# Four graph layers on one core: in the GAT walks SyncE copies 12 of turn 54's 14 columns row by row, and the staging of gather indices goes

## The chip, the cores and the metric

One NeuronCore of a Trainium2 chip runs the whole program. The metric is device time in microseconds, the median of several executions; lower is better. The engines are TensorE, VectorE (DVE), ScalarE (ACT), GpSimd (POOL) and SyncE (SP), each with its own queue of instructions; 16 DMA engines move data between the HBM and the on-chip memory (SBUF).

## The reference

Four graph neural network layers are applied in turn to 6250 nodes with 128 features and 100,000 edges (`src`, `dst`, sorted by `dst`), each with a residual and a layer norm:

```
x = layernorm(x + L0(x, src, dst))                  # gated sum of x[dst]-x[src]
x = layernorm(x + L1(x, src, dst, edge_weight))     # 4-head attention, aggregated at src
x = layernorm(x + L2(x, edge_index, edge_attr))     # 8-head attention with edge bias, and a feed-forward
x = layernorm(x + L3(x, edge_index))                # two GAT layers, 4 heads each
```

A GAT layer computes `h = x @ W`, a score for each edge and head `e = leaky_relu(a_src(h)[src] + a_dst(h)[dst])`, a softmax of `e` over the edges of one `dst`, and the sum of `h[src] * alpha` over them. Each node also counts as a neighbour of itself.

## The kernel before, in words

The program has five phases of edge work (`ph` 0 to 4; phases 3 and 4 are the two GAT layers) and a last, sixth pass over the nodes. A phase begins with dense work on the nodes, in 7 groups of 7 x 128 nodes: it reads the sums of the phase before, normalizes, multiplies by the weights and writes two tables to HBM: `table[ph]`, one row a node with what an edge needs of its `src` (in the GAT phases 136 floats, 544 bytes: 4 heads of 33 and 4 scores), and `dst_table[ph]`, with what it needs of its `dst`. Then the phase walks over the edges.

The edges lie in chunks: partition p of 128 holds the 784 edges p*784 to p*784+783 in order, padded at the end (`CH` = 784). A walk goes in `NG` = 56 turns of `B` = 14 columns; column c of all partitions is 128 edges. Since edges are sorted by `dst`, a sum over one node is a running sum along a partition, cut where `cont` is 0.

**One turn.** GpSimd issues one indirect DMA for each column (L725): it takes 128 row numbers, one a partition, and fetches 128 rows of `table[ph]` into `rows`, which holds two slots of 14 columns. Turn g uses slot g % 2. The 14 gathers of a turn add to `rows_landed[s]`, on which VectorE waits (L2114). Before it issues turn g, GpSimd waits at L719 for the turn's indices, and at L720 until the turn that used the slot before is done with it (`rows_used`). In the GAT phases VectorE then adds the scores and forms a running maximum (L2135 to L2142), ScalarE takes exponentials (L1227), VectorE multiplies the rows by them into PSUM and runs one scan of 1980 columns (L2104), ScalarE copies the result to `sums` (L1242) and prepares the gates of the next turn (L1204), and issues the store of the running sums to `states[ph]` (L1248). The helper that issues most VectorE operations stands at L1285, L1293 and L1296, so many rows of the profile have these lines.

**Indices.** The row numbers of all 784 columns lie in the tile `src` from the start of the program. Before a walk ScalarE copies the 14 columns of turns 0 and 1 into the two halves of a tile `idx` (L1199 to L1201), and in each turn g, once `rows_used` has reached g + 3, those of turn g + 2 (L1238, L1239), counted in `idx_staged`. `src` has 28 columns of padding for the last two.

**Phases 0 and 2** have wider rows (256 and 264 floats), and SyncE also loads, turn by turn, the rows of the `dst` side (L588 to L591); VectorE works longer in a turn than in the GAT phases. In phase 0 VectorE also builds one-hot tiles (`hotS`, `hotSH`) with which TensorE counts the edges by source; ScalarE multiplies the rows there (L1221) and is the one to report `rows_used`. Phase 1 has no gathers by `table`: it scatters the edges into the order of `src` and reads them back.

**SyncE** issues in phase 3 and 4: the stores of the 7 groups of both tables (L553, L555), then, when the spreading of the `dst` table to edges has ended (L581), one load of 1.6 MB into `dflat` (L585), after which it goes on to the next phase, where it waits for the first table group (L551). In the last pass it stores the output (L560 to L566).

**The end of a walk.** After turn 55 GpSimd waits for the last stores (L729), fetches the boundary rows (L732), and VectorE, TensorE and ScalarE join the partial sums of a node that spans two partitions; `msg` holds an operand there (L2239). GpSimd writes the rows back (L735), and the next phase's dense work starts with gathers by node (L655).

Of the kernel before, what the change touches and what calls it, by code (L numbers as in the profile page):

```python
# [5 lines left out]
I32 = mybir.dt.int32  # L6
BF16 = mybir.dt.bfloat16
ALU = mybir.AluOpType
ACT = mybir.ActivationFunctionType
# [4 lines left out]
D = 128  # L14
P = 128
# [18 lines left out]
TURN = {0: 0, 2: 1, 3: 2, 4: 3}  # L34

# [29 lines left out]
def build(nc, a, out):  # L65
    with ExitStack() as ctx:  # L66
# [31 lines left out]
        src = sb("src", [P, CH + 2 * B], I32)  # L98
# [27 lines left out]
        idx = sb("idx", [P, 2, B], I32)  # L126
# [62 lines left out]
        hotSH = hot_turned(ebuf, 0, NB)  # L189
        early_hotS = [hotS, hot_turned(ebuf, 2240, P)]  # L190
        early_hotSH = [hotSH, hot_turned(ebuf, 2240 + ntile // 2, NB)]
# [59 lines left out]
        ssums = [sums[:, 0:B * 136], sums[:, B * 136:2 * B * 136], dflat[:, 1792:1792 + B * 136]]  # L251

# [100 lines left out]
        first1_end = sem("first1_end")  # L353
# [7 lines left out]
        idx_staged = sem("idx_staged")  # L361
# [75 lines left out]
        def scattered_at(ph, g):  # L437
            turns = -(-(KG - g % ZS) // ZS)
            return 16 * KB * (ph * turns + g // ZS + 1)

# [11 lines left out]
        def _(sp):  # L452
# [93 lines left out]

            for ph in range(6):
# [36 lines left out]
                if ZW[ph] == 4:  # L584
                    sp.dma_start(dflat[:, 0:CH * 4], view.rearrange("p c d -> p (c d)")).then_inc(slim_in, 16)  # L585

                if ZW[ph] == ROW:
                    for g in range(NG):  # L588
# [3 lines left out]
                        if ph == 1 and g < NG - 1:  # L592
                            low_digits(g + 1)
                if ph == 0:
# [19 lines left out]
        def _(pool):  # L614
# [52 lines left out]
            for ph in range(6):  # L667
# [32 lines left out]
                if ph == 1:  # L700
# [5 lines left out]
                                            bass.IndirectOffsetOnAxis(ap=fixi[:, 2:3], axis=0)).then_inc(first1_end, 16)  # L706
# [3 lines left out]
                else:  # L710
# [5 lines left out]
                    for it in range(IT):  # L716
                        for s in range(2):
                            g = it * 2 + s
                            pool.wait_ge(idx_staged, g + (1 + TURN[ph] * (NG + 2)))  # L719
                            pool.wait_ge(rows_used, g + (1 + TURN[ph] * NG))  # L720
                            if g == 1 and ph < 3:
                                spreads_landed()
                            for j in range(B):
                                at = (s * B + j) * GW[ph]
                                pool.indirect_dma_start(rows[:, at:at + GW[ph]], None, table[ph][:, :],  # L725
                                                        bass.IndirectOffsetOnAxis(ap=idx[:, s, j:j + 1], axis=0)).then_inc(rows_landed[s], 16)
# [245 lines left out]
        def _(act):  # L972
# [91 lines left out]
            for ph in range(6):  # L1064
# [133 lines left out]
                else:  # L1198
# [1084 lines left out]
```

## Time and profile before

| what | value |
|---|---|
| median of 3 runs | 7559.2 us (7523.48, 7559.2, 7564.5) |
| profiled execution: span from first to last instruction | 6570.3 us |
| profiled execution's own time | not printed; the median lies 988.9 us above the span |
| instructions in the span | 37158 |
| VectorE, GpSimd, ScalarE, TensorE busy | 4654.6, 4293.2, 1375.2, 1251.3 us |
| first and last gather of the phase 3 walk start at | 4325.30 and 5310.16 us |
| first and last gather of the phase 4 walk start at | 5470.30 and 6454.64 us |

How to read the profile: a row names a line of the kernel, an engine and an operation, then the tile it writes and those it reads, and how many instructions it stands for. "Idle before" is the time for which the engine had nothing to run just ahead of them, with what ended it. Register, branch and semaphore instructions and the issuing of DMAs are not counted as busy; SPq and ACTq are the queues from which SyncE and ScalarE issue DMAs. "Issue" means that the engine waited for nothing that the profile shows.

### The profile page before, as it was taken

To read this page: it belongs to the slowest core of one execution; us is meant where nothing else is said; L and a number is where in the kernel's file an instruction comes from. 1 tells how busy PE (TensorE), PEld (TensorE's weight loads), DVE (VectorE), ACT (ScalarE), POOL (GpSimd) and SP (SyncE) were. 2 spreads that over 40 slices of the span, in tenths; PEclk is the share of its full clock that TensorE was granted. 3 is DMA by queue.
4 is the path that set the end of the run, shared out by engine and by line. 5 is a ranking of instruction groups with operands and counts; after the bars stand their busy time and mean duration, and the time that the engine had idled before them with its cause. 6 is when DMAs were issued, how large, how long until landed. Compare 5 with 4: busy or idle time off the path is not lost. (4 is left out here: it accounts for less than half of the span.)

```text
span 6570.3 us, 37158 instructions
## 1 busy us (share of the span) xinstructions
PE 1251.3 (19%) x8049; PEld 1094.3 (17%) x8049; DVE 4654.6 (71%) x9455; ACT 1375.2 (21%) x3580; POOL 4293.2 (65%) x4445
## 2 busy tenths in 40 slices
PE   7100000145555534332000000810000010000000
PEld 6100000135544433322000000610000010000000
DVE  7788888799999969987888887744444444444445
ACT  0122222220111114431000000622222211222223
POOL 0777777667777760027777775367777767777775
PEclk9555555555555555556555555955555555555555
DMA  9666666433443437754666664123333323333332
GB/s 391 199 218 202 202 199 204 130 106 131 132 136 133 133 115 292 295 184 153 220 219 218 225 218 158 30 85 109 113 111 109 115 74 90 112 113 109 113 111 82
DMA packets 338944, 1032.97 MB, mean 157 GB/s; under 512 B 100325, under 2 KB 163137, under 8 KB 331294
## 3 DMA queue, kind: packets, MB, share of 16 engines
q0 software_dynamic: 166752, 401.68, 21.4%
q1 hardware_dynamic: 116642, 342.34, 14.8%
q10 hardware_dynamic: 55324, 286.57, 12.1%
q8 instruction: 63, 1.03, 0.1%
q14 instruction: 163, 1.34, 0.1%
HBM read 602.97 MB, written 427.39 MB: 157 GB/s over the span
## 5 line engine op out<-in xcount | busy, mean ns | idle before, releaser
L725 POOL DMA_INDIRECT rows<-table,idx x3136 | 2987.4, 953 | 985.0 <-issue 973.1
L644 POOL DMA_INDIRECT by_src<-ebuf,place x784 | 767.4, 979 | 275.0 <-issue 238.3
L1296 DVE SCALAR_TENSOR_TENSOR psA<-psA,cont,dstf 128x128 f32<-128x128 f32 (+1 forms) x2349 | 836.6, 356 | 48.0 <-ACT ebuf L1025 27.2
L1285 DVE TENSOR_TENSOR sc<-rows,ebuf 128x56 f32<-128x56 f32 x112 | 28.2, 252 | 1023.9 <-DMA rows<-table,idx 1023.9
L958 PE MATMUL psA<-dstf,ones 128*128 128x512 f32 x10 | 9.9, 1113 | 3055.3 <-DVE dstf L2223 3055.3
L1296 DVE SCALAR_TENSOR_TENSOR sums<-sums,cont,psA 128x128 f32<-128x128 f32 (+1 forms) x1512 | 518.9, 343 | 30.3 <-ACT psA L1221 29.0
L958 PEld LDWEIGHTS psA<-dstf,ones 128*128 128x128 f32 x10 | 2.7, 317 | 3056.9 <-issue 3056.9
L823 PE MATMUL psA<-attr,sums 128*128 128x49 f32 x1568 | 406.1, 403 | 470.8 <-DVE attr L1475 470.8
L2104 DVE TENSOR_TENSOR_SCAN psA<-rows,psA 128x1980 f32<-128x1980 f32 x112 | 480.0, 4286 | 3.9
L823 PEld LDWEIGHTS psA<-attr,sums 128*128 128x128 f32 x1568 | 397.0, 326 | 476.9 <-DVE attr L1475 476.9
L1227 ACT ACTIVATE psA<-df 128x60 f32<-128x60 f32 (+1 forms) x168 | 40.4, 241 | 1714.2 <-DVE df L1285 1714.2
L1285 DVE TENSOR_TENSOR psA<-rows,psA 128x1848 f32<-128x1848 f32 (+1 forms) x168 | 352.8, 2100 | 0.2
L732 POOL DMA_INDIRECT fixr<-states,fixi x5 | 5.0, 995 | 518.1 <-DMA states<-sums 464.6
L1285 DVE TENSOR_TENSOR rows<-rows,psA 128x1792 bf16<-128x1792 bf16 (+3 forms) x118 | 231.1, 1958 | 111.1 <-DMA rows<-table,idx 104.3
L655 POOL DMA_INDIRECT sums<-states,nidx x245 | 256.4, 1046 | 81.0 <-issue 72.2
L663 POOL DMA_INDIRECT spread_wide<-rows,nidx x147 | 159.8, 1087 | 215.2 <-DVE rows L1285 165.2
L1242 ACT ACTIVATE sums<-psA 128x1848 f32<-128x1848 f32 x112 | 191.5, 1710 | 459.8 <-DVE psA L2104 459.8
L1285 DVE TENSOR_TENSOR rows<-psA,rows 128x1792 f32<-128x1792 f32 (+2 forms) x168 | 203.2, 1210 | 118.6 <-DMA rows<-table,idx 107.0
L1023 ACT ACTIVATE ebuf<-psA 128x1792 f32<-128x1792 f32 x56 | 94.1, 1681 | 904.4 <-DMA by_src<-ebuf,place 784.6
L795 PE MATMUL psA<-ebuf 128*128 128x49 bf16 x588 | 63.5, 276 | 965.2 <-DVE ebuf L1285 965.2
L1221 ACT ACTIVATE psA<-rows,wt 128x128 f32<-128x128 f32 x784 | 233.0, 352 | 33.7 <-DVE wt L2124 33.7
L795 PEld LDWEIGHTS psA<-ebuf 128*128 128x128 bf16 x588 | 54.5, 144 | 974.1 <-DVE ebuf L1285 974.1
(350 smaller groups left out, 5533.6 us busy)
## 6 DMA issues: line engine op xcount, KB each, us to landing
dstf<-spread_wide SPq DMA_DIRECT2D x168, 924.0 KB
states<-sums ACTq DMA_DIRECT2D x150, 952.0 KB, 4.0
rows<-by_src SPq DMA_DIRECT2D x55, 1035.0 KB, 5.1
states<-sums ACTq DMA_DIRECT2D x56, 1008.0 KB, 5.7
spread_wide<-sums SPq DMA_DIRECT2D x56, 924.0 KB, 24.7
states<-sums ACTq DMA_DIRECT2D x56, 903.0 KB, 7.4
rows<-table,idx POOLq DMA_INDIRECT x3136
msg<-low_rows SPq DMA_DIRECT2D x56, 448.0 KB, 3.7
```

Source lines behind the costliest of these rows:

```text
L644: pool.indirect_dma_start(by_src[:, :], bass.IndirectOffsetOnAxis(ap=place[:, s, j:j + 1], axis=0), payload[:, s, j, :], None).then_inc(so ...
L655: pool.indirect_dma_start(nrows[g % NS][:, b * w:(b + 1) * w], None, states[ph - 1][:, :], bass.IndirectOffsetOnAxis(ap=nidx[:, order, k:k ...
L663: pool.indirect_dma_start(spread[ph][:, :], bass.IndirectOffsetOnAxis(ap=nidx[:, 1, k:k + 1], axis=0), zslot(ph, g)[:, b * ZW[ph]:(b + 1) ...
L725: pool.indirect_dma_start(rows[:, at:at + GW[ph]], None, table[ph][:, :], bass.IndirectOffsetOnAxis(ap=idx[:, s, j:j + 1], axis=0)).then_i ...
L795: m = pe.matmul(cells, hotS[:, :, j], hotSH[:, :, j], start=False, stop=True, skip_group_check=True)
L823: pe.matmul(t, hotT[s][:, j, :], cell[:, :, j], start=True, stop=False)
L1023: act.activation(payload[:, s, :, 0:ROW].rearrange("p b (h d) -> p b h d", d=33)[:, :, :, 0:32], heldS[:, :, 0:D].rearrange("p b (h d) -> ...
L1221: m = act.activation(gated[:, j * D:(j + 1) * D], rows[:, at:at + D], ACT.Copy, scale=wt[:, s, j:j + 1])
L1242: act.activation(S3[:, :, 0:F], chain_msg.rearrange("p (f b) -> p b f", b=B + 1)[:, 1:B + 1, :], ACT.Copy).then_inc(states_turned, 1)
L1285: return dve.tensor_tensor(o_, a_, b_, op)
L1296: return dve.scalar_tensor_tensor(o_, a_, s_, b_, op0, op1)
L2104: tell(dve.tensor_tensor_scan(chain_msg, chain_gate, chain_msg, 0.0, ALU.mult, ALU.add), su)
```

## The change

`SIDE` = 54 and `SIDE_COLS` = {3: 12, 4: 12}: in the phases 3 and 4, turn 54 is not gathered into a slot of `rows` but into a tile of its own, `msg`. Of its 14 columns SyncE copies the first 12: for each partition it loads 12 row numbers from `src` into registers with one instruction, and for each of them issues a DMA of one row of `table[ph]`, whose address comes from the register, to the place of that row in `msg`; each adds 16 to `side_landed[ph]`, and VectorE waits for all 1536 before turn 54. It starts when the tables are saved and X is kept (`side_open`), behind the load at L585. GpSimd gathers the other two columns, after turn 53's. The remaining 55 turns take the two slots of `rows` in turn, so that turn 55 uses slot 0 (`row_slot`, `free_at`, `landed_at`). Phases 0 and 2 have no such turn.

In all four walks the gathers take their indices straight from `src`: `idx`, `idx_staged`, ScalarE's copies and the padding of `src` go, and GpSimd waits once before a walk for `src` and for `n_kept` (X copied), and before a turn for `rows_used` alone. `hotSH` of the late turns of phase 0 moves from `ebuf` to `msg`; `first1_end` is merged into `first_end`. The tables `side_tile` for phases 0 and 2 are not used.

```diff
@@ -32,6 +32,8 @@
 ROW = 132
 ITEM = 138
 TURN = {0: 0, 2: 1, 3: 2, 4: 3}
+SIDE = 54
+SIDE_COLS = {3: 12, 4: 12}


 HEADS = [1, 4, 8, 4, 4]
...
-        early_hotSH = [hotSH, hot_turned(ebuf, 2240 + ntile // 2, NB)]
+        early_hotSH = [hot_turned(ebuf, 0, NB), hot_turned(ebuf, 2240 + ntile // 2, NB)]
         mark = ebuf[:, numbers_at + ntile // 2:numbers_at + ntile // 2 + CH]
         ex = df
...
+        side_tile = {0: ebuf, 2: aux[:, :, :].rearrange("p b d -> p (b d)"), 3: msg, 4: msg}

         psA = ctx.enter_context(nc.psum_tensor("psA", [P, 4096], F32))
...
             turns = -(-(KG - g % ZS) // ZS)
             return 16 * KB * (ph * turns + g // ZS + 1)

+        def row_slot(ph, g):
+
+            side = SIDE if ph in SIDE_COLS else NG
+            return None if g == side else (g - int(g > side)) % 2
+
+        def slot_turns(ph, s, g=NG):
+
+            return sum(row_slot(ph, k) == s for k in range(g))
+
+        def landed_at(ph, g):
+
+            s = row_slot(ph, g)
+            before = sum(slot_turns(q, s) for q in TURN if q < ph)
+            return 16 * B * (before + slot_turns(ph, s, g) + 1)
+
+        def side_gathered_at(ph):
+
+            return 16 * sum(B - n for q, n in SIDE_COLS.items() if q <= ph)
+
+        def free_at(ph, g):
+
+            s = row_slot(ph, g)
+            users = [k for k in range(g) if row_slot(ph, k) == s]
+            return 2 + TURN[ph] * NG + (users[-1] + 1 if users else 0)
+
+        def turn_rows(ph, g):
+
+            s = row_slot(ph, g)
+            tile = side_tile[ph][:, 0:B * GW[ph]] if s is None else rows[:, s * B * GW[ph]:(s + 1) * B * GW[ph]]
+            return tile.rearrange("p (b w) -> p b w", b=B)
+
         FIRST_LOADS = 6
         LOADS = len(BIAS) - 2 + 5 + 10 + 4
...
                 sp.dma_start(attr[P - 1:P, s, :], attr_tail.rearrange("(p c) d -> p (c d)", p=1)[:, at]).then_inc(attr_landed[s], 16)

+            numbers_of = [sp.alloc_register(f"side_row{j}") for j in range(B)]
+
+            def side_open(ph):
+
+                sp.wait_ge(src_in, 48)
+                if ph == 0:
+                    sp.wait_ge(chains_ready, 1)
+                    sp.wait_ge(bias3_ready, 1)
+                    for k in range(2):
+                        sp.wait_ge(tab_first[k], 16 * -(-(KG - k) // 2))
+                else:
+                    sp.wait_ge(tab_saved, 16 * KG * TURN[ph])
+                    sp.wait_ge(n_kept, (2 if ph == 2 else 3) * KG)
+
+            def side_rows(ph, parts):
+
+                w, at, n = GW[ph], SIDE * B, SIDE_COLS[ph]
+                for p in parts:
+                    sp.load(numbers_of[0:n], src[p:p + 1, at:at + n])
+                    for j in range(n):
+                        node = sp.snap(numbers_of[j])
+                        sp.dma_start(side_tile[ph][p:p + 1, j * w:(j + 1) * w], table[ph][bass.ds(node, 1), :]).then_inc(side_landed[ph], 16)
+
             for ph in range(6):

...
                     sp.wait_ge(diag_done, 1)
                 if ZW[ph] == 4:
                     sp.dma_start(dflat[:, 0:CH * 4], view.rearrange("p c d -> p (c d)")).then_inc(slim_in, 16)
+                    side_open(ph)
+                    side_rows(ph, range(P))

                 if ZW[ph] == ROW:
...
+                        if ph in SIDE_COLS and g == 1:
+                            side_open(ph)
+                        if ph in SIDE_COLS and 1 <= g < SIDE - 1:
+                            side_rows(ph, range((g - 1) * P // (SIDE - 2), g * P // (SIDE - 2)))
                 if ph == 0:
                     sp.wait_ge(ends1_copied, 1)
...
@@ -713,17 +776,23 @@
                             pool.wait_ge(tab_first[k], 16 * -(-(KG - k) // 2))
                     else:
                         pool.wait_ge(tab_saved, 16 * KG * TURN[ph])
-                    for it in range(IT):
-                        for s in range(2):
-                            g = it * 2 + s
-                            pool.wait_ge(idx_staged, g + (1 + TURN[ph] * (NG + 2)))
-                            pool.wait_ge(rows_used, g + (1 + TURN[ph] * NG))
-                            if g == 1 and ph < 3:
-                                spreads_landed()
-                            for j in range(B):
-                                at = (s * B + j) * GW[ph]
-                                pool.indirect_dma_start(rows[:, at:at + GW[ph]], None, table[ph][:, :],
-                                                        bass.IndirectOffsetOnAxis(ap=idx[:, s, j:j + 1], axis=0)).then_inc(rows_landed[s], 16)
+                    pool.wait_ge(src_in, 48)
+                    if ph:
+                        pool.wait_ge(n_kept, (2 if ph == 2 else 3) * KG)
+                    for g in range(NG):
+                        s = row_slot(ph, g)
+                        if s is None:
+                            for j in range(SIDE_COLS[ph], B):
+                                pool.indirect_dma_start(side_tile[ph][:, j * GW[ph]:(j + 1) * GW[ph]], None, table[ph][:, :],
+                                                        bass.IndirectOffsetOnAxis(ap=src[:, g * B + j:g * B + j + 1], axis=0)).then_inc(side_gathered, 16)
+                            continue
+                        pool.wait_ge(rows_used, free_at(ph, g))
+                        if g == 1 and ph < 3:
+                            spreads_landed()
+                        for j in range(B):
+                            at = (s * B + j) * GW[ph]
+                            pool.indirect_dma_start(rows[:, at:at + GW[ph]], None, table[ph][:, :],
+                                                    bass.IndirectOffsetOnAxis(ap=src[:, g * B + j:g * B + j + 1], axis=0)).then_inc(rows_landed[s], 16)

                     for s in range(2):
...
                 if ph == 1:
                     payloads()
                     sorted_pass()
-                else:
-                    act.wait_ge(rows_used, 2 + TURN[ph] * NG)
-                    for s in range(2):
-                        act.activation(idx[:, s, :], src[:, s * B:(s + 1) * B], ACT.Copy).then_inc(idx_staged, 1)
...
-                                at = (s * B + j) * GW[0] + D
-                                m = act.activation(gated[:, j * D:(j + 1) * D], rows[:, at:at + D], ACT.Copy, scale=wt[:, s, j:j + 1])
+                                m = act.activation(gated[:, j * D:(j + 1) * D], turn_rows(0, g)[:, j, D:2 * D], ACT.Copy, scale=wt[:, s, j:j + 1])
                                 if j in MSG_PARTS[:-1]:
...
-                        act.wait_ge(rows_used, g + (3 + TURN[ph] * NG))
-                        act.activation(idx[:, s, :], src[:, bass.ds((g + 2) * B, B)], ACT.Copy).then_inc(idx_staged, 1)
                         act.wait_ge(sums_ready, g + (1 + ph * NG))
...
                     for s in range(2):
                         g = it * 2 + s
                         ahead = not (last and s)
-                        G3 = rows[:, s * B * GW[ph]:(s + 1) * B * GW[ph]].rearrange("p (b w) -> p b w", b=B)
+                        G3 = turn_rows(ph, g)
                         S3 = sums[:, s * B * W:(s + 1) * B * W].rearrange("p (b w) -> p b w", b=B)
                         Sp = sums[:, ((2 - s) * B - 1) * W:(2 - s) * B * W]
                         ce = bass.ds(g * B, B)
-                        dve.wait_ge(rows_landed[s], it * (16 * B) + (16 * B + TURN[ph] * IT * 16 * B))
+                        if row_slot(ph, g) is None:
+                            dve.wait_ge(side_landed[ph], 16 * P * SIDE_COLS[ph])
+                            dve.wait_ge(side_gathered, side_gathered_at(ph))
+                        else:
+                            dve.wait_ge(rows_landed[row_slot(ph, g)], landed_at(ph, g))
                         if ph == 0:
                             G1 = G3[:, :, 0:D]
```

## Rows read from the trace of the kernel before

**Rows 1.** The page's head: span, busy times, memory throughput in 40 slices.

```profile
span 6570.3 us, 37158 instructions
...
PE 1251.3 (19%) x8049; PEld 1094.3 (17%) x8049; DVE 4654.6 (71%) x9455; ACT 1375.2 (21%) x3580; POOL 4293.2 (65%) x4445
...
GB/s 391 199 218 202 202 199 204 130 106 131 132 136 133 133 115 292 295 184 153 220 219 218 225 218 158 30 85 109 113 111 109 115 74 90 112 113 109 113 111 82
```

**Rows 2.** Busy time by stretch; the walks of phases 0, 2, 3 and 4.

```profile
core 0: us, PE busy (x) PEld busy (x) DVE busy (x) ACT busy (x) POOL busy (x), PEclk, DMA share, GB/s
221.00:1240.00 1019.00, 62.01 (x574) 53.19 (x574) 843.45 (x1968) 257.45 (x880) 760.92 (x785) 0.50 0.61 203
3064.00:4060.00 996.00, 0.00 (x0) 0.00 (x0) 848.87 (x2002) 55.19 (x277) 742.12 (x784) 0.50 0.66 217
4325.00:5323.00 998.00, 0.00 (x0) 0.00 (x0) 447.18 (x459) 232.57 (x389) 742.35 (x784) 0.50 0.38 110
5470.00:6468.00 998.00, 0.00 (x0) 0.00 (x0) 447.28 (x459) 232.56 (x389) 742.21 (x784) 0.50 0.38 110
```

**Rows 3.** Waits, 4325 to 5323 us: who waited for whom, total, times, longest.

```profile
DVE sc L1285 <- DMA rows<-table,idx: 512.2, 56, 10.2
...
POOL rows L725 <- issue: 243.8, 784, 1.3
```

**Rows 4.** Groups of instructions, 4325 to 5323 us: busy, mean ns, idle before.

```profile
L725 POOL DMA_INDIRECT rows<-table,idx x784 | 742.4, 947 | 243.8 <-issue 243.8
...
L1239 ACT ACTIVATE idx<-src 128x14 int32<-128x14 int32 x56 | 12.0, 214 | 113.0 <-DVE psA L1285 113.0
```

**Rows 5.** Timeline, start of the phase 3 walk: start, length, what [idle before].

```profile
4324.87 0.33 SPq L585 DMA_DIRECT2D dstf<-spread_slim  x1
4325.30 0.96 POOL L725 DMA_INDIRECT rows<-table,idx  x1 [0.30 <-issue]
4326.56 0.94 POOL L725 DMA_INDIRECT rows<-table,idx  x1 [0.30 <-issue]
```

**Rows 6.** Timeline, end of the phase 3 walk: turns 53, 54 and 55.

```profile
5277.08 0.25 DVE L1285 TENSOR_TENSOR sc<-rows,ebuf 128x56 f32<-128x56 f32 x1 [9.25 <-DMA rows<-table,idx]
...
5278.95 0.94 POOL L725 DMA_INDIRECT rows<-table,idx  x1 [1.16 <-issue]
...
5281.15 4.29 DVE L2104 TENSOR_TENSOR_SCAN psA<-rows,psA 128x1980 f32<-128x1980 f32 x1
...
5295.29 0.25 DVE L1285 TENSOR_TENSOR sc<-rows,ebuf 128x56 f32<-128x56 f32 x1 [9.86 <-DMA rows<-table,idx]
...
5299.36 4.29 DVE L2104 TENSOR_TENSOR_SCAN psA<-rows,psA 128x1980 f32<-128x1980 f32 x1
...
5310.16 0.94 POOL L725 DMA_INDIRECT rows<-table,idx  x1 [0.30 <-issue]
5312.76 0.25 DVE L1285 TENSOR_TENSOR sc<-rows,ebuf 128x56 f32<-128x56 f32 x1 [9.12 <-DMA rows<-table,idx]
```

**Rows 7.** Waits of SyncE's DMA queue, whole run: total, times, longest.

```profile
SPq L553 <- DVE aux L1296: 1414.9, 14, 1044.3
SPq L560 <- ACT X L1121: 1086.3, 6, 1040.1
```

**Rows 8.** One line's instructions, L545: duration ns min/median/max, first and last start.

```profile
L545 SPq DMA_DIRECT2D attr<-attr_tail x56: 227/332/585, 2454.5 to 2868.9; - x56
```

**Rows 9.** Timeline, 130 to 137 us: SyncE's three stores of one row each.

```profile
133.47 0.81 SPq L513 DMA_DIRECT2D states<-small  x1
133.82 5.22 ACTq L993 DMA_DIRECT2D table<-rows  x1
...
134.34 0.66 SPq L514 DMA_DIRECT2D states<-small  x1
...
135.04 0.69 SPq L515 DMA_DIRECT2D states<-small  x1
```

**Rows 10.** Timeline of SyncE's queue, phase 1: two DMAs, then one.

```profile
2502.76 0.93 SPq L544 DMA_DIRECT2D attr<-in_edge_attr  x2
2503.73 0.33 SPq L545 DMA_DIRECT2D attr<-attr_tail  x1
```

**Rows 11.** Waits of GpSimd, whole run: total, times, longest.

```profile
POOL rows L725 <- ACT idx L1239: 9.5, 4, 2.4
```

**Rows 12.** Timeline, phase 0: one of the four turns that waited.

```profile
742.05 0.21 ACT L1239 ACTIVATE idx<-src 128x14 int32<-128x14 int32 x1
...
742.76 0.94 POOL L725 DMA_INDIRECT rows<-table,idx  x1 [2.36 <-ACT idx L1239]
```

**Rows 13.** One line's instructions, L1153: ScalarE's copies into X.

```profile
L1153 ACT ACTIVATE X<-rows x4: 952/954/954, 4158.4 to 4304.9; 128x896 f32<-128x896 f32 x4
```

More of the change, by code:

```diff
@@ L97, in build @@
         aux = sb("aux", [P, NB, 136])
-        src = sb("src", [P, CH + 2 * B], I32)
+        src = sb("src", [P, CH], I32)
         cont = sb("cont", [P, CH])
@@ L125, in build @@
         attr = sb("attr", [P, 2, B * 32])
-        idx = sb("idx", [P, 2, B], I32)
         cg = sb("cg", [P, 2, B])
@@ L188, in build @@
         hotS = hot_turned(ebuf, numbers_at + ntile // 2, P)
-        hotSH = hot_turned(ebuf, 0, NB)
+        hotSH = hot_turned(msg, 1024, NB)
         early_hotS = [hotS, hot_turned(ebuf, 2240, P)]
-        early_hotSH = [hotSH, hot_turned(ebuf, 2240 + ntile // 2, NB)]
+        early_hotSH = [hot_turned(ebuf, 0, NB), hot_turned(ebuf, 2240 + ntile // 2, NB)]
         mark = ebuf[:, numbers_at + ntile // 2:numbers_at + ntile // 2 + CH]
@@ L352, in build @@
         ends1_saved = sem("ends1_saved")
-        first1_end = sem("first1_end")
         diag1_ready = sem("diag1_ready")
@@ L360, in build @@
         dve_step = sem("dve_step")
-        idx_staged = sem("idx_staged")
+        side_landed = {p: sem(f"side_landed{p}") for p in SIDE_COLS}
+        side_gathered = sem("side_gathered")
         rows_landed = [sem(f"rows_landed{s}") for s in range(2)]
@@ L705, in _ @@
                     pool.indirect_dma_start(firstk[:, 0:1], None, ends_src[:, :],
-                                            bass.IndirectOffsetOnAxis(ap=fixi[:, 2:3], axis=0)).then_inc(first1_end, 16)
+                                            bass.IndirectOffsetOnAxis(ap=fixi[:, 2:3], axis=0)).then_inc(first_end, 16)
                     pool.wait_ge(order_ready, 1)
@@ L1768, in sorted_pass @@
                     if g == 4:
-                        dve.wait_ge(first1_end, 16)
+                        dve.wait_ge(first_end, 32)
                         link(tt(chunkf[:, 1:2], firstk[:, 0:1], chunkf[:, 0:1], ALU.min))
```

## The prediction

> **What bounds the kernel now.** I first read the page's head and busy times [rows 1]. VectorE has the largest total (71% of the span), GpSimd the next (65%), so the totals decide nothing and the stage has to be looked at. The table by stretch comes next [rows 2]: in the two GAT walks (4325 to 5323 and 5470 to 6468 us) VectorE works 447 of 998 us, ScalarE 233, TensorE nothing, and the DMA engines 0.38 of the time, while GpSimd has its 784 gathers. The waits of the first walk say who holds whom [rows 3]: VectorE waits 512.2 us for gathered rows, in all 56 turns, and GpSimd waits for nothing but its own issue. The groups of that walk give the price [rows 4]: a gather is 0.947 us, and 243.8 us of idle time lie before the 784, 0.31 each. So a GAT walk lasts as long as GpSimd takes to issue gathers. From the first start to the last, 4325.30 to 5310.16 [rows 5, 6], there are 783 steps in 984.86 us: 1.258 us a gather, extra gaps such as the 1.16 us at 5278.95 included.
>
> SyncE is free there. Its queue issues one DMA at 4324.87 [rows 5] and then waits 1044.3 us for the next phase's first table rows, and 1040.1 us for the output in the second walk [rows 7].
>
> **The change, part by part.**
>
> *Gathers removed.* In each GAT walk GpSimd issues 2 of turn 54's 14 gathers: 12 x 1.258 = 15.1 us less. They stand on the path, since everything after them moves forward: the last gather starts at 5295.07 instead of 5310.16, and VectorE opens turn 55 at 5297.67 instead of 5312.76 [rows 6]. Two walks: 30.2 us.
>
> *Turn 54 on VectorE.* It ran from 5295.29 to 5303.65 (the scan at 5299.36 plus 4.29), 8.36 us [rows 6]. Turn 53's scan ends at 5285.44, so there is room for it before 5297.67 provided that it starts by 5289.31. Its two own gathers follow turn 53's at once and land by then. Its rows now lie in msg, which no turn of these phases uses; that part costs nothing. So the tail of the walk (turn 55, its store, the repair of boundary rows) keeps its length.
>
> *SyncE's copies.* This is the new work: 128 partitions x 12 rows = 1536 copies in each walk, 128 loads of 12 numbers into registers, and the register steps of each address. They begin behind the DMA of 4324.87, at 4325.20 [rows 5]: the other three waits of side_open (src loaded, table saved, X kept) are over when GpSimd begins. With 2.60 us from the last issue to VectorE's start (5310.16 to 5312.76 [rows 6], borrowed from the gathers), they must be issued in 5289.31 - 4325.20 - 2.60 = 961.5 us. That is **0.626 us a row** for the full gain. At 961.5 + 15.1 = 976.6 us, 0.636 a row, the gain is gone; beyond it each further 0.01 us costs 15.4 us a walk.
>
> What does a row cost? The nearest rows are SyncE's one-row copies of attr_tail (1.8 KB): 0.227 least, 0.332 median, 0.585 most [rows 8]. Three one-row stores at 133 to 135 us, beside table stores and the clearing of spread_wide, took 0.66 to 0.81 us [rows 9]. The GAT walks have a DMA share of 0.38, so I take the median, 0.332. Between two issues of SyncE lie 0.04 us (2502.76 + 0.93 to 2503.73 [rows 10]), which I count as one sequencer step. The address of a row from a register needs more steps, and no row shows one: from 0.04 (one step) to 0.30 (GpSimd's issue gap before each gather [rows 5]); I take four steps, 0.16, since they are sequencer work as the 0.04 is. The load of 12 numbers is not in the trace either: at least one step, at most a whole trip as a DMA's 2.60 us, that is 0.003 to 0.22 a row; I take 0.05. Sum: 0.332 + 0.04 + 0.16 + 0.05 = **0.58 us a row**, 891 us a walk, 70 us early. The ends: 0.227 + 0.04 + 0.04 + 0 = 0.31 and 0.81 + 0.04 + 0.30 + 0.22 = 1.37.
>
> The Trainium skill, "Runtime: NRT & Kernel Launch", section "Instruction fetch mechanics", has a price for register loads: about 200 ns a register even in bulk. No row here shows a register load. By it the load alone is 0.20 a row, the row an estimated 0.73, and the copies come late; it says this of registers loaded from HBM, and here they come from SBUF.
>
> *Index staging gone.* In the GAT walks ScalarE's 56 copies of 0.214 us lie in its waits [rows 4], and GpSimd waited for none of them; zero. In phase 0 GpSimd waited for idx 4 times [rows 11]. At 742.76 it had waited 2.36 us, of which the copy itself is 0.21 (from 742.05 [rows 12]); the rest is the wait for the rows to be used, which stays. I count 0.3 x 4 = 1.2 us; at least 0, at most the 0.71 from the copy's start to GpSimd's, 2.8 in all. Phase 2 is issue-bound and had no such wait.
>
> *Nothing:* the shorter src tile, the histogram's one-hot tile in msg instead of ebuf (same operation, same size), one semaphore fewer at first_end, and GpSimd's added waits at the start of a phase (ScalarE's last copy into X starts at 4304.9 [rows 13], 20 us ahead). If that cover went, the wait would delay the first gather of a walk by as much.
>
> **The sum.** 30.2 + 1.2 = 31.4 us. The span would go from 6570.3 to 6538.9. The profiled execution's own time is not printed; the span lies 988.9 us under the median of the three runs, 7559.2, and I take that as unchanged. Forecast **7528 us** (-0.4%).
>
> **The rivals.**
>
> *A. SyncE is late (slower).* DVE's wait for side_landed in turn 54 takes the place of the wait for the gathers, with turn 55, its store, GpSimd's repair gathers and all of the next phase behind it. It decides from 0.636 us a row. With the one-row stores of 0.69 plus 0.05 [rows 9], 0.74 a row without any register work, a walk is 1536 x 0.74 - 976.6 = 160 us longer: 7559 + 320 = 7879. For it: two parts of the row's price are unseen and the margin is 8%. Against it: those stores ran against a DMA system moving 391 GB/s in the page's first slice, and the GAT walks move 110 [rows 1, 2]. At 0.65 it is 7559 + 2 x 21.8 - 1 = 7602.
>
> *B. The part outside the span grows with the program.* If the 988.9 us go with the number of instructions, 988.9 / 37158 = 0.027 us each [rows 1], the 3072 copies and 256 loads (less 256 removed) add 3072 x 0.027 = 82 us: 7528 + 82 = 7610. Nothing on the page ties that part to anything.
>
> *C. The copies go one after the other.* If each must land before the next begins on its DMA queue, a row costs 2.60 us and a walk 3994 us: 7559 + 2 x 3017 = 13,590. Against it: gathers start every 1.25 us and land 2.6 us after their issue, so landings overlap [rows 5, 6]. The Trainium skill, "DMA: Bandwidth & Descriptors", sections "Anatomy of one DMA" and "Rules for kernel authors", gives a fixed 2.0 us for each DMA and advises to coalesce transfers under 64 KB; a page's estimate for 1536 in series would be 3072 us. The overlap of the gathers speaks against the series, not against the 2.0.
>
> *D. The copies slow the gathers.* If the shared DMA engines stretched a gather by 2%, 0.025 x 1544 = 39 us would be lost: 7528 + 39 = 7567. In phases 0 and 2, at a share of 0.61 and 0.66, the engine time of a gather is much as in the GAT walks (760.9 and 742.1 us for 785 and 784, against 742.4 [rows 2]), so I hold little of it.
>
> **How the numbers follow.** Forecast holds 0.68; A 0.19; B 0.06; C 0.01; D 0.06. A measurement of this kernel can tell about 0.5% from no change: 7521 to 7597. The forecast, 0.4% below, lies inside; with the three runs' own spread (-36 to +5 us) I give it 0.24 faster and 0.44 same. A gives 0.14 slower and 0.05 same, B 0.04 slower and 0.02 same, D 0.06 same, C 0.01 slower. Faster 0.24, same 0.57, slower 0.19. Range 7495 to 7610: below by the spread of the runs and the 2.8 us bound, above through D and A up to 0.65 us a row.
>
> **What would show it.** Right: 772 gathers by GpSimd in each GAT walk; turn 55 opened about 972 us after the first gather (987.5 before); SyncE's 1536 copies over before some 964 us; the mean distance of two copies under 0.626 us; no wait of turn 54 on side_landed. Wrong: a VectorE wait in turn 54 released by SyncE's copies (A), the span shorter by 31 us and the time not (B), gathers longer than 0.95 us (D). The forecast falls if a copy with its steps takes over 0.636 us.

## The result, and the profile after

| | before | after |
|---|---|---|
| median of the timed runs | 7541.3 us (4 runs, 7492.8 to 7564.5) | 8799.3 us (4 runs, 8784.4 to 8854.2) |
| ratio, 95% interval | | 1.170 [1.163, 1.177] |
| profiled execution, its own time and span | 6570.3 us span | 8809.1 us, 8807.3 us span |

17% slower; the forecast was 7528 us, and 8799 lies far outside the range. One thing must be said ahead of everything else: a time here depends on the chip. The same kernel before took 6569.9 and 6586.8 us (medians of 19 and 7 runs) on two of the chips met below and 7596.2 and 7509.7 us (11 and 13 runs) on two others. By its span, the trace of before that the prediction was made from comes from a chip of the first kind; the times of 7523 to 7564 us and all that the table has of after come from the second. I call them the 6.6 ms chips and the 7.5 ms chips; gains and losses are compared within one chip only.

The head of the page of after, and its memory throughput, against [rows 1]:

```profile
span 8807.3 us, 46163 instructions
...
PE 1281.1 (15%) x8049; PEld 1111.7 (13%) x8049; DVE 4691.4 (53%) x9455; ACT 1325.1 (15%) x3348; POOL 4389.3 (50%) x4421
...
GB/s 333 184 176 168 167 170 114 97 96 107 110 103 100 213 295 143 178 182 187 180 179 117 25 109 103 99 99 79 1 1 13 77 107 99 98 103 39 1 1 40
```

Its own time, 8809.1, is 1.8 us above its span: nothing to speak of lies outside the span. No engine but SyncE has much more work than before (VectorE is busy for 4691 us against 4655, GpSimd 4389 against 4293, in a span longer by 2237). But twice the DMA engines move 1 GB/s for two slices of 220 us in a row. The waits of the whole run say who waits there, and the table by stretch (walk, hole, walk) how much stands still; they answer to [rows 2, 3]:

```profile
DVE sc L1348 <- DMA msg<-table: 1362.9, 2, 684.3
```

```profile
5061.00:6114.00 1053.00, 0.00 (x0) 0.00 (x0) 431.23 (x442) 214.45 (x324) 793.63 (x771) 0.50 0.36 103
6114.00:6800.00 686.00, 0.00 (x0) 0.00 (x0) 15.17 (x16) 4.30 (x8) 1.09 (x2) 0.50 0.01 3
6956.00:8010.00 1054.00, 0.00 (x0) 0.00 (x0) 431.40 (x442) 214.44 (x324) 793.95 (x771) 0.50 0.36 103
```

VectorE waits twice, 681 us on average, for rows that SyncE copies into msg (`side_landed`). In the 686 us behind the first walk's gathers it works 15 us. The chain of work that ended last has SyncE's three new lines at its head, 24% of the span:

```profile
SPq L602 16%; SPq L601 5%; SPq L599 3%; POOL sums L718 1%; PE psA L942 1%; DVE rows L1348 0%; PE psA L954 0%; PE psA L929 0%; DVE psA L2167 0%; PE psA L813 0%; DVE small L1635 0%; PE psA L918 0%; DVE psA L1348 0%; ACT rows L1161 0%
```

What one row costs SyncE is seen in the instructions of line 602 alone: count, duration in ns (least, median, most), first and last start. First for 5100 to 5700 us, with gathers beside them, then for 6140 to 6700, with none:

```profile
L602 SPq MOVE msg<-table x140: 4/699/1398, 5100.4 to 5698.9; - x140
L602 SPq DMA_DIRECT2D msg<-table x140: 3/699/1398, 5101.8 to 5699.6; - x140
...
L602 SPq DMA_DIRECT2D msg<-table x1089: 1/225/697, 6139.9 to 6699.9; - x182
L602 SPq MOVE msg<-table x1088: 29/29/688, 6141.3 to 6699.9; - x182
```

A row is three instructions: a fused register operation (L601), a move and the DMA (L602), and for every 12 rows a load (L599). Without gathers 1089 rows take 560 us, 0.51 each. Beside gathers 140 rows take 600 us, 4.3 each, and the median of a register move, 29 ns elsewhere, is 699 ns. By the last gather's time 283 of 1536 rows are issued; the other 1253 take from 6114.0 to 6780.7, 0.53 each, and that is the hole. Both walks together: with the holes closed, 8807.3 - 1362.9 = 7444 us, near before's span on such a chip (7491.3 us below).

### The profile page after: what moved, and what is told of

It reads as the page before. It is cut to its first block and busy times, and to the rows that moved or that the text cites. A ratio compares the mean times of both kernels' runs of the same rounds, so it can differ in the third digit from the quotient of the medians.

```text
span 8807.3 us, 46163 instructions
## 1 busy us (share of the span) xinstructions
PE 1281.1 (15%) x8049; PEld 1111.7 (13%) x8049; DVE 4691.4 (53%) x9455; ACT 1325.1 (15%) x3348; POOL 4389.3 (50%) x4421
## 3 DMA queue, kind: packets, MB, share of 16 engines
q8 instruction: 63, 1.03, 0.0%
## 5 line engine op out<-in xcount | busy, mean ns | idle before, releaser
L794 POOL DMA_INDIRECT rows<-table,src x3108 | 3082.7, 992 | 1367.1 <-issue 995.6
L1348 DVE TENSOR_TENSOR sc<-msg,ebuf 128x56 f32<-128x56 f32 x2 | 0.5, 253 | 1362.9 <-DMA msg<-table 1362.9
L864 PE MATMUL psA<-msg,ebuf 128*128 128x49 bf16 x588 | 63.4, 276 | 1140.0 <-DVE msg L1348 1029.7
```

Of the source, the lines that this page charges most:

```text
L1348: return dve.tensor_tensor(o_, a_, b_, op)
```

## The experiments

**What separates the theories.** Either register addresses are dear on SyncE as such, or SyncE is held by something beside it: by the instruction or by the DMA. And either the change brought the 7.5 ms with it, or they were there before.

**Before once more, and the change without the copies.** On a 6.6 ms chip (before 6569.9 us, 19 runs). The second kernel has the new indices and no turn 54 of its own:

```
-SIDE_COLS = {3: 12, 4: 12}
+SIDE_COLS = {}
...
-                    side_open(ph)
-                    side_rows(ph, range(P))
+                    if ph in SIDE_COLS:
+                        side_open(ph)
+                        side_rows(ph, range(P))
```

> The kernel before, unchanged, to have its trace under the same conditions as the changed kernel's. The trace of before spans 6570 us, its timed runs 7541, and the changed kernel's span (8807) equals its time. If the timed runs of before are slow outside the GAT walks too, the span here is 7490 to 7570, the walk of phase 0 takes about 1178 us as after the change (1012 in the first trace), and the GAT walks start near 5060 us. If the 971 us lie outside the span, the span is 6570 again and the changed kernel lost 735 us before its first GAT walk by the change itself.

> The changed kernel with no side columns: GpSimd gathers all 14 columns of all turns by indices taken straight from src, and SyncE copies nothing. Theory A (SyncE's copies are the whole loss): 7541 us of before within 0.3%, so 7520 to 7560, GAT gathers 1.26 us apart. Rival (direct indices or the moved one-hot tile slow phases 0 to 2): 8200 to 8300 us, that is 735 us slower than before.

Measured: before in one execution 6587.9 us, its span 6586.1. Neither of the two expectations holds: 1.8 us lie outside the span here too, and time and span are both short, so the chip is of another kind than the one that was timed. The direct indices took 6571.5 us (10 runs), ratio 1.0001 [0.9992, 1.0011]; the 7520 to 7560 us expected were for the other kind of chip, and only the ratio can be held against them. The index staging was worth nothing that 0.1% can show, and it is not the loss.

**One column, and rows at fixed addresses.** Same chip. The first leaves SyncE one column (128 rows, each with a load of its own). The second copies 1536 rows that are known beforehand, with no load and no register step; the attention of turn 54 is then over other rows than the edges name.

```
-SIDE_COLS = {3: 12, 4: 12}
+SIDE_COLS = {3: 1, 4: 1}
```

```
-                    sp.load(numbers_of[0:n], src[p:p + 1, at:at + n])
...
-                        node = sp.snap(numbers_of[j])
-                        sp.dma_start(..., table[ph][bass.ds(node, 1), :])...
+                        sp.dma_start(..., table[ph][p * 12 + j:p * 12 + j + 1, :])...
```

> The changed kernel with one side column a walk instead of 12: 128 copies by SyncE, 13 gathers by GpSimd in turn 54. While GpSimd gathers, the changed kernel's SyncE issued a row each 4.2 us. Theory A: 128 rows take some 540 us, ready before turn 54 is due at 961, no wait for side_landed, and the time is within 0.5% of before. Rival (the copies slow the gathers from 1.26 to 1.37 us whatever else): the gathers are slowed only while rows are issued, so some 40 us a walk are lost, +80 us or 1%.

> The changed kernel with its 1536 copies a walk, but each from a fixed row of the table: no load of numbers, no register steps. It leaves out the lookup of the 12 side columns, so those rows are not those of the edges. Theory H1 (beside the gathers each instruction of SyncE is held for about 1.4 us, whatever it does): one instruction a row instead of three, 1.4 us a row, 1536 rows in 2150 us beside gathers, or some 750 rows by the gathers' end and the rest at 0.27 us: walk about 1054 + 210 = 1270 us, total some 7541 + 2 x 250 = 8050. Theory H2 (the DMA alone is slow, 4.2 us a row): as the changed kernel, 8800. Theory H3 (the register load and the register address are slow): 0.27 us a row, in time, 7510 us.

One column: 6568.4 us (8 runs), ratio 0.9998 [0.9987, 1.0008], its 2.5 us too small to be seen; fixed rows in a single execution: 6541.6 us, 28.3 under before's median and 46.3 under its single execution above. That is in time, as theory H3 has it, but on this chip it decides nothing between H1, H2 and H3: they were made for the 7.5 ms chip. The instructions of one line in each; of the column the loads and the copies in the whole run, of the fixed rows the first walk:

```profile
L599 SPq TENSOR_LOAD <-src x256: 429/507/1404, 4335.1 to 5610.5; - x128
...
L602 SPq DMA_DIRECT2D msg<-table x256: 254/255/326, 4335.7 to 5611.2; - x128
```

```profile
L600 SPq DMA_DIRECT2D msg<-table x1536: 214/252/1124, 4324.6 to 4820.7; - x192
```

Beside gathers, on this chip, 1536 copies are issued in 496 us, 0.323 a row. So the copies can be in time, and SyncE isn't held to 1.4 us an instruction there; how large the gain is, one execution can't tell (four runs below give it). The load of one number is 0.507 us.

**After again, with 14 and with 6 columns.** On a 7.5 ms chip (before 7596.2 us, 11 runs).

```
-SIDE_COLS = {3: 12, 4: 12}
+SIDE_COLS = {3: 14, 4: 14}   (the second kernel; the third has 6)
```

> The changed kernel, unchanged, timed beside before on a chip where before takes 6570 us. Theory H4 (the copies are in time where SyncE's instructions run at their own pace, and late only where they are held): fixed rows took 0.32 us each beside the gathers; with register steps of 0.044 and 0.029 us and a load of 1.02 us for 12 rows, about 0.5 to 0.55 us a row, 770 to 850 us of the 961 there are, no wait for side_landed, and 6541 us (-0.43%), as e4. Rival H5 (the copies from register addresses are held by the gathers themselves, 4.2 us a row): 7700 us or more, with a wait of some 680 us in each walk.

> The changed kernel with all 14 columns of turn 54 copied by SyncE, 1792 rows a walk. H4: a row costs 0.5 to 0.55 us, 900 to 985 us, at the edge of the 944 us left (961.5 less two more gathers... the window shrinks to some 5289 - 4325 - 2.6 - 2.5 = 959): between 6536 (in time) and 6590. H5: worse than e5, 8000 us or more.

> The changed kernel with 6 side columns: 768 copies a walk, 8 gathers in turn 54. H4: in time by far; half the gain of twelve, 2 x 6 x 1.258 = 15.1 us: 6555 us. H5: 768 rows at 4.2 us take 3225 us beside the gathers, or some 230 by their end and 540 more at 0.5: walk 270 us longer, 7110 us.

| columns by SyncE | us | ratio | two waits for msg, us |
|---|---|---|---|
| 6 | 8268.1 (4 runs) | 1.086 [1.082, 1.091] | 693.1 |
| 12 | 8933.9 (6 runs) | 1.175 [1.172, 1.178] | 1371.3 |
| 14 | 9255.7 (4 runs) | 1.216 [1.211, 1.220] | 1685.9 |

The chip hoped for didn't come, so the figures of H4 and H5 in these three texts, made for a 6.6 ms chip, were not tested. The loss repeats, and it is the wait: each run stands above before by about what VectorE waits for msg (672 against 693, 1338 against 1371, 1660 against 1686). From 6 to 14 columns the loss grows by 123 us a column in two walks, 0.48 us a row: each further row is one more to issue after the gathers, at nearly the 0.53 us that a row took there. On such a chip half the columns lose too.

**Before, after, fixed rows and register work alone, side by side.** On another 7.5 ms chip (before 7509.7 us, 13 runs). The third has the fixed rows of above. The fourth has no side copies (direct indices); in both walks SyncE does the 128 loads of 12 numbers and adds them up, and then copies one row whose address comes from the sum:

```
+                        for p in range(P):
+                            sp.load(numbers_of[0:12], src[p:p + 1, SIDE * B:SIDE * B + 12])
+                            for j in range(12):
+                                sp.reg_add(total, total, numbers_of[j])
```

> The kernel before, unchanged, for its trace beside the next three. On a chip where before is timed near 6570 us it shows nothing new. On one where it is timed near 7600: theory H6 (there the engines' instructions are held in steps of 0.7 us while GpSimd gathers) has the scans and multiplications of phases 0 and 2 spaced by 1.4 us in stretches, GpSimd's gathers unheld at 1.25 us, and the GAT walks some 100 us longer than 985.

> The changed kernel beside before and e10 on one chip. Where before takes 6570 us: a row costs 0.5 to 0.55 us, in time, 6541 us (H4). Where it takes 7600 us: 8930 us as in e5.

> e4 again on the same chip as e9: 1536 copies a walk from fixed rows, one instruction a row instead of three, no register loads; the 12 side columns are not looked up. Where before takes 6570 us: 6541 us. Where it takes 7600 us: H1/H6 (each SyncE instruction held about 1.4 us beside gathers) has about 750 rows out at the gathers' end, the other 790 at 0.3 us: 230 us late in each walk, 8050 us. H2 (only the DMAs are held, 4.2 us each): 8700 us or more.

> No side columns (GpSimd gathers all 14), but in each GAT walk SyncE does the 128 loads of 12 numbers and 12 register additions for each, and no copies except one at the end. Nobody waits for SyncE before the next phase's tables. If what is slow is the copies: same time as before within 0.5% on any chip. If SyncE's instructions beside the gathers hold the other engines up: slower than before by 1% or more where before takes 7600 us, with gathers over 1.3 us apart in the GAT walks.

Measured: before 7493.1 in one execution, its span 7491.3; after 8826.3 us (4 runs), 1.175 [1.167, 1.183]; fixed rows 7954.9 us (4 runs), 1.061 [1.054, 1.068]; register work alone 7503.0 us (10 runs), 0.998 [0.994, 1.002].

The trace of before on this chip is the one I should have had. Its table by stretch has the same stages as [rows 2], and a stage of phase 1 in the middle:

```profile
236.00:1408.00 1172.00, 62.41 (x577) 53.48 (x576) 855.68 (x1967) 257.33 (x880) 753.77 (x783) 0.50 0.53 175
2951.00:3365.00 414.00, 164.03 (x642) 133.83 (x641) 392.91 (x1395) 183.15 (x796) 0.00 (x0) 0.50 0.80 295
3572.00:4751.00 1179.00, 0.00 (x0) 0.00 (x0) 860.77 (x1972) 54.60 (x275) 741.12 (x784) 0.50 0.56 182
5059.00:6130.00 1071.00, 0.00 (x0) 0.00 (x0) 439.38 (x450) 230.20 (x385) 798.58 (x784) 0.50 0.35 103
```

The trace of the prediction has this for the stage in the middle:

```profile
2455.00:2869.00 414.00, 164.20 (x643) 134.01 (x641) 392.54 (x1394) 183.16 (x796) 0.00 (x0) 0.50 0.80 295
```

From first to last gather, the walk of phase 0 is 1172.5 us here against 1012.3, that of phase 2 1179.0 against 985.9, a GAT walk 1070.9 against 984.9, with much the same busy time of VectorE. The four walks hold 526 of the 921 us between the two spans. Most of the rest lies in phase 1, ahead of the stage in the middle, where GpSimd scatters with 784 indirect DMAs (L644, idle before them 576.3 us against 275.0). The stage of phase 1 in which GpSimd does nothing lasts 414 us on either chip, though VectorE is busy there for 393 us, TensorE for 164 and the DMA engines move 295 GB/s. So these chips are slow where GpSimd issues its indirect DMAs, and not in the one long stage without them. TensorE's clock is no part of it: granted 0.50 in all these stretches on either chip.

Of theory H6 half came true: a GAT walk is 86 us longer (expected some 100), but the gathers are not unheld at 1.25 us; they are 1.37 us apart in the mean. And the kernel before is slow there too: on this chip it reaches its first GAT walk at 5058.9 us, the fixed rows at 5059.8 and after at 5097.2, 38 us apart where before's own times spread over 117 us. The change did not bring the 7.5 ms.

How SyncE is held is read from the first GAT walk of the three changed kernels on this chip, until the gathers end or the work is done:

| kernel | SyncE's instructions | in us | each |
|---|---|---|---|
| after, 5097 to 6152 | 24 loads, 287 fused, 287 moves, 287 DMAs: 885 | 1055 | 1.19 |
| fixed rows, 5060 to 6114 | 825 DMAs | 1054 | 1.28 |
| register work, 5110.8 to 5554.5 | 128 loads, 256 fused: 384 | 443.7 | 1.16 |

Rows of the three, one fence each; of after, the copies alone:

```profile
L602 SPq DMA_DIRECT2D msg<-table x287: 2/699/1398, 5098.6 to 6151.8; - x144
```

```profile
L600 SPq DMA_DIRECT2D msg<-table x825: 3/700/1401, 5060.0 to 6113.7; - x165
```

```profile
L651 SPq FUSED_REGOPS  x256: 2/698/1399, 5111.8 to 5553.1; - x128
...
L649 SPq TENSOR_LOAD <-src x128: 3/700/1399, 5110.8 to 5551.0; - x128
```

Whatever the instruction is, a register operation, a load or a DMA, SyncE gets through one in some 1.2 us in the mean (gathers are 1.37 us apart here), with durations heaped at 0.7 and 1.4 us. One instruction a row in place of three therefore gets 825 rows out in the time of 287, close to the 750 that theory H1 had, and the time of 7954.9 close to its 8050, while the 8700 us or more of H2 are ruled out; the waits for msg fall from 1358.7 to 494.8 us and the loss from 1317 to 445 us. So it is not the DMA that is dear but each instruction, and SyncE's register work holds nobody else up by more than 0.6% (0.998, interval from 0.994). The same run has the direct indices and no side copies, so on this kind of chip too the loss comes with the copies. At 1.2 us an instruction about 280 rows, with three instructions each, fit into a walk, two columns, worth at most 2 x 1.37 us a walk; such a kernel would be too near to before to be told from it and has no run here. None of these kernels beats before on such a chip.

**After and fixed rows on a 6.6 ms chip.** Every time of after up to here is from a 7.5 ms chip, so whether the forecast holds on the other kind is open. These two ran on one with before at 6586.8 us (7 runs).

> The changed kernel once more, in the hope of the kind of chip on which before takes about 6570 us. There, theory 1 (SyncE's instructions are held beside GpSimd's gathers only on the chips where before takes 7500 us and more): a row costs 0.5 to 0.6 us (the 0.323 of a fixed copy plus 0.044 and 0.029 and 0.085 of the load), the 1536 copies take 770 to 920 us of the 961 there are, no wait in turn 54, and the kernel stands about 28 us under before (ratio 0.9957). Theory 2 (register addresses are dear beside gathers on every chip): rows of 1 us and more as with a load each, so a walk is 560 us or more longer and the ratio 1.15 or more. On a chip of the other kind both give 1.17 to 1.18 as in the two earlier runs.

> The fixed-address kernel (the copies read rows that are constants, so no loads and no register steps; the attention of turn 54 is then over other rows) beside the changed one on the same chip. Where before takes about 6570 us: theory 1 and theory 2 both 6542 (ratio 0.9957), as in its one look there; this gives it an interval. On a chip of the other kind: 1.06 as before, and the difference from the changed kernel (0.11) is again the price of the two register instructions a row and the load.

Measured: after 6555.0 us (4 runs, 6549.9 to 6558.9), ratio 0.995 [0.993, 0.997]; fixed rows 6550.7 us, 0.995 [0.993, 0.996]. The change gains here, 31.8 us by the medians, as theory 1 has it; theory 2, 1.15 or more, is out. Register addresses cost the time next to nothing. SyncE's instructions in the first walk of after:

```profile
L602 SPq MOVE msg<-table x1536: 29/29/38, 4336.4 to 5176.7; - x192
L602 SPq DMA_DIRECT2D msg<-table x1536: 224/225/983, 4336.5 to 5176.8; - x192
...
L599 SPq TENSOR_LOAD <-src x128: 952/1028/2843, 4335.3 to 5170.9; - x128
```

All 1536 rows are out in 841.7 us (4335.3 to 5177.0), 0.548 each, with gathers beside them all the time. The end of the walk, GpSimd first and then VectorE; it answers to [rows 6]:

```profile
5285.98 0.94 POOL L794 DMA_INDIRECT rows<-table,src  x1 [0.31 <-issue]
5287.23 0.95 POOL L786 DMA_INDIRECT msg<-table,src  x1 [0.30 <-issue]
5288.48 0.94 POOL L786 DMA_INDIRECT msg<-table,src  x1 [0.30 <-issue]
...
5305.98 0.94 POOL L794 DMA_INDIRECT rows<-table,src  x1 [0.30 <-issue]
```

```profile
5292.69 4.29 DVE L2167 TENSOR_TENSOR_SCAN psA<-rows,psA 128x1980 f32<-128x1980 f32 x1
5297.01 0.25 DVE L1348 TENSOR_TENSOR sc<-msg,ebuf 128x56 f32<-128x56 f32 x1
...
5300.56 0.30 DVE L1348 TENSOR_TENSOR psA<-sums,psA 128x132 f32<-128x132 f32 x1 [2.15 <-ACT psA L1292]
...
5302.88 4.29 DVE L2167 TENSOR_TENSOR_SCAN psA<-rows,psA 128x1980 f32<-128x1980 f32 x1
5308.61 0.25 DVE L1348 TENSOR_TENSOR sc<-rows,ebuf 128x56 f32<-128x56 f32 x1 [1.45 <-DMA rows<-table,src]
```

Turn 54 begins with no wait, straight behind turn 53's scan; it is 120 us too late to catch SyncE at it.

## Why the prediction was wrong

**The sum held, on the kind of chip it was made from.** Forecast -31.4 us; measured there -31.8, with an interval of -22 to -43. That they agree to 0.4 us is luck: the gathers account for 27.1 of it in the trace, and the interval is 21 us wide.

- *Gathers removed*, forecast 15.1 us a walk: the first gather starts at 4334.9, the last at 5306.0, 971.1 us where there were 984.9 [rows 5, 6], so 13.8, and 13.3 in the second walk. The last gather moved up by less than twelve steps because the others took 1.260 us and not 1.258. Right to about a tenth.
- *Turn 54 on VectorE*, forecast 8.36 us with room: it took 10.16 (5297.01 to 5307.17), because it now follows turn 53 at once and waits 2.15 us for ScalarE's exponentials, whose engine first copies out turn 53 and prepares the next gates. Turn 55 still waits 1.45 us for its gathers, so the cover held, by less than I thought.
- *SyncE's copies*, forecast 0.58 us a row, 70 us early: 0.548 and 120 early. The parts were off and cancelled. The copy is 0.225 (I took 0.332), the register steps 0.044 + 0.029 (0.16), the load 1.03 / 12 = 0.086 (0.05), all medians, which leaves 0.164 for gaps (0.04) and for what is longer than its median. The rule of the Trainium skill, "Runtime: NRT & Kernel Launch", section "Instruction fetch mechanics", of some 200 ns a register, doesn't hold for this load: 0.086 a register, 12 at a time from SBUF. It says it of loads from HBM.
- *Index staging*, forecast 1.2 us: 1.0001 in the interval of 0.1%, too small to be seen. The rival D, gathers slowed by the copies: 0.947 us in the median against 0.944, and 1.260 us from gather to gather against 1.258. Not so.
- *Rival C*: rows 0.55 us apart, not 2.6, and 0.53 on the other kind of chip when no gathers run beside them; beside them a row takes 4.3 us there, but rows from fixed addresses 1.28, so it isn't the landing that is waited for. The 2.0 us that the prediction takes from the Trainium skill, "DMA: Bandwidth & Descriptors", section "Anatomy of one DMA", stands there for DMAs issued by GpSimd; no run here shows it for SyncE's.

**The step that failed** is the price of SyncE's row, 0.58 us, and with it the "70 us early" and the wait for side_landed that the sum puts at nothing. On the chips that were timed a row takes 4.3 us beside the gathers and 1.12 us in the average of a walk; VectorE waits 1362.9 us in two walks, and that is the loss. Behind it stands the step in "The sum": "the span lies 988.9 us under the median of the three runs, 7559.2, and I take that as unchanged", with the part outside the span. There is no such part: span and time of an execution differ by 1.7 to 1.8 us in the runs above. The 989 us were inside the span, on a chip that executes the walks and the scatter more slowly, as the trace of before from such a chip shows, and my durations were those of the other kind of chip. Rival B took the same premise further and falls with it; it also counted 3072 new instructions where the trace has 9005 (46163 - 37158), so that its own price would have been some 240 us and not 82. A gap of 13% between the trace and the times was the largest unexplained number in front of me, larger by 30 times than the change; it was booked as a constant when it should have been read as: the timed executions have other durations than these rows, and I don't know which.

**Rival A is what happened there**, at a higher price: 1536 rows from 5062.5 to 6780.7 are 1.12 us a row on average, where the rival was priced at 0.74 and the row's upper end was 1.37; the 4.3 beside the gathers stand nowhere in it. Its place (VectorE's wait in turn 54, everything behind it late), its sign and its point of decision were right; 0.19 was too little for a case that decides at 8% of margin. The rows that I priced the copy by [rows 8, 9] come from stages where GpSimd issues no gathers, and on the 7.5 ms chip line 545 is unchanged as well (343 ns against 332 in the median, in that same stage of 414 us). So no row of SyncE's from a walk stood behind the 0.58, and even on that other chip those rows would have warned of nothing; the lengths of the walks would have.

## What to carry to other kernels

Before a change of 0.4% is priced, the span of the trace has to be held against the timed runs: if they differ by far more than one execution's time and span do (1.8 us here), the durations in the trace aren't those that are timed, and no row of it can decide a margin of 8%. Work moved to an idle queue should be counted in instructions too, not only in bytes or DMAs: with one instruction a row instead of three the loss here fell by two thirds, and beside the gathers of a 7.5 ms chip a load of 12 numbers was held as long as the move of one (both 0.70 us in the median). A hidden helper that must be done by a fixed time wants a reserve for the slowest chip it runs on; 12 columns had 12% on one kind of chip and were short by a factor of five on the other.

## What the runs showed of the hardware

- The same program takes 6.57 to 6.59 ms on two chips and 7.51 to 7.60 on two others, with the same busy time of VectorE (4654.6 and 4685.7 us); the difference lies in the stages in which GpSimd issues indirect DMAs, and the one long stage without them is equal to the microsecond.
- On the slower chips a SyncE instruction beside gathers takes 1.2 us on average, be it a register move of 29 ns. VectorE's short instructions are held too: in the walk of phase 2 on such a chip 87 of them (L1296) stand behind gaps of 0.9 us on average, where the first trace has no such wait:

```profile
DVE psA L1296 <- remote: 78.9, 87, 1.7
```

- "Remote" says that the releaser isn't in the trace, in a program with one core. The traces of the slower chips lack most of their semaphore records in just those stages: of before, 31,353 updates in all where the first trace has 95,665, 1751 in a GAT walk against 14,193, but 5242 against 5227 in the stage of 414 us without gathers. So what a wait there is put down to is less sure than its length.
- What in these chips holds the instructions no run could tell. The Trainium skill, "NOTIFIC — the notification-queue block", section "Overflow: three behaviours, one of which stalls the engine", says that the internal pipeline of the trace records pushes back rather than lose a record inside the block, and that a full ring either drops records or stalls who makes them. Missing records and held instructions in the same stages would fit that; that the one causes the other isn't shown, nor that these chips are slow when nothing is recorded.
- On the 6.6 ms chips a load of 12 numbers from SBUF into SyncE's registers takes 1.03 us in the median, of one 0.51. There a one-row copy costs SyncE 0.323 us from issue to issue at a fixed address and 0.548 at a register address, everything counted.
